# Image 0 in three transfers over 128 partitions, sums of the first cells by identity products, and zeros ahead of image 0

## The reference

```
# first layer
g    = relu(bn2(einsum('nchw,oc->nohw', x, wg1))).mean(axis=(2, 3))
xg0  = (relu(tanh(g @ wg2.T + bg2)) + beta)[0]            # of image 0 alone
p    = round(xg0[:31] / xg0.sum() * 96)                   # splits the channels among 32 filters
filt = basis[i] for channels between param[i] and param[i+1]
xp   = x.reshape(n, 96, 7, 8, 7, 8).mean(axis=(3, 5))     # 7 x 7 cells of 8 x 8 pixels
y    = relu(bn1((xp * filt).sum(axis=(2, 3)) @ w1d[:, :, 1].T + b1d))
x    = x * y + x
# second layer
t    = relu(gamma * (x.mean(axis=(2, 3)) @ w1.T - mean) * rsqrt(var + eps) + beta)
wt   = (t @ w2.T + b2) as 3 x 3 for each image and channel, masked to its first four taps
out  = depthwise conv of x with wt + bias
```

## Time and profile before

| | |
|---|---|
| time, median of 3 runs | 230.43 us (229.45 to 232.28) |
| profiled execution, time | 229.69 us |
| its span, first to last instruction | 227.5 us |
| mean granted TensorE clock | 0.954 of full speed |
| busy: PE, PEld | 206.4 us, 119.0 us |
| busy: DVE, ACT, POOL | 199.4 us, 132.4 us, 129.5 us |
| DMA | 79.05 MB, mean 348 GB/s |
| largest group | L740 PE, 480 records, 171.1 us |

### The profile page before, as it was taken

The page is one execution under the profiler, slowest core; times in us unless marked ns, Lnnn a source line. Parts: engine busy times, 40 slices in busy tenths (PEclk is TensorE's granted clock), DMA queues, the critical chain, the costliest instruction groups (busy, mean ns, idle before and its releaser), DMA issues.

```text
span 227.5 us, 2390 instructions
## 1 busy us (share of the span) xinstructions
PE 206.4 (91%) x742; PEld 119.0 (52%) x742; DVE 199.4 (88%) x216; ACT 132.4 (58%) x190; POOL 129.5 (57%) x121
## 2 busy tenths in 40 slices
PE   7291866999999999999999999999999999999991
PEld 3141453556556555655565656565556555655550
DVE  6036969997999999999999999989999999788983
ACT  2002115648765867586767677667766775687650
POOL 3004167998598669867886878696879400040000
PEclk9769585999999999999999999999999999999999
DMA  4999999869999999999999999999997246615676
GB/s 109 276 426 430 426 430 421 354 192 353 430 375 405 371 415 432 426 355 426 437 422 357 424 432 424 389 413 422 383 419 335 124 176 282 282 71 212 282 309 256
DMA packets 8155, 79.05 MB, mean 348 GB/s; under 512 B 1040, under 2 KB 1072, under 8 KB 2128
## 3 DMA queue, kind: packets, MB, share of 16 engines
q1 hardware_dynamic: 8144, 78.92, 86.7%
HBM read 40.38 MB, written 38.54 MB: 347 GB/s over the span
## 4 chain that ended last, share of the span: by engine, by line
PE 75%; DVE 10%; ACT 6%; DMA 3%; issue 2%; SPq 1%; DVEq 1%; ACTq 0%
PE banks L740 61%; DVE banks L550 6%; ACT banks L625 4%; PE banks L688 3%; DMA xout<-x 3%; PE banks L725 2%; PE banks L732 2%; PE banks L711 2%; PE banks L713 2%; DVE xout L550 2%; PE banks L675 1%; ACT diag L620 1%; DVE stats L425 1%; SPq L284 1%; PE banks L703 1%
## 5 line engine op out<-in xcount | busy, mean ns | idle before, releaser
L740 PE MATMUL banks<-xin,diag 128*128 128x385 f32 (+1 forms) x480 | 171.1, 507 | 3.0 <-ACT banks L625 2.7
L740 PEld LDWEIGHTS banks<-xin,diag 128*128 128x128 f32 x480 | 88.4, 192 | 68.4 <-issue 27.2
L339 POOL TENSOR_TENSOR halves<-xin 128x1568 f32<-128x1568 f32 (+2 forms) x22 | 74.1, 3371 | 43.9 <-DVE stats L438 21.3
L550 DVE SCALAR_TENSOR_TENSOR banks<-xin,coef,banks 128x1485 f32<-128x1485 f32 x48 | 84.8, 1768 | 6.9 <-ACT banks L625 6.3
L625 ACT ACTIVATE banks<-xin,wide_sb,coef 128x784 f32<-128x784 f32 (+2 forms) x71 | 84.3, 1207 | 10.6 <-DVE xout L559 8.8
L550 DVE SCALAR_TENSOR_TENSOR xout<-xin,coef,banks 128x1485 f32<-128x1485 f32 x24 | 42.2, 1758 | 0.6 <-issue 0.3
L646 ACT ACTIVATE xout<-banks 128x784 f32<-128x784 f32 x24 | 19.8, 824 | 39.2 <-PE banks L740 39.2
L344 POOL TENSOR_TENSOR halves<-halves 128x784 f32<-128x784 f32 x18 | 33.2, 1845 | 1.4
L620 ACT ACTIVATE diag<-wide_sb,coef 128x128 f32<-128x128 f32 x72 | 23.5, 389 | 5.9 <-DVE coef L484 5.9
L559 DVE SCALAR_TENSOR_TENSOR xout<-xin,coef,banks 128x825 f32<-128x825 f32 x24 | 25.6, 1067 | 1.0 <-PE banks L740 0.8
L366 POOL TENSOR_TENSOR edges<-xin,coef 128x84 f32<-128x84 f32 x24 | 8.3, 344 | 21.0 <-DVE coef L484 20.2
(11 more groups left out here) (72 smaller groups left out, 77.2 us busy)
## 6 DMA issues: line engine op xcount, KB each, us to landing
xin<-x SPq DMA_DIRECT2D x23, 1568.0 KB, 10.9
out<-xout SPq DMA_DIRECT2D x23, 1568.0 KB, 13.0
xout<-x SPq DMA_DIRECT2D x4, 294.0 KB, 5.3
xin<-x SPq DMA_DIRECT2D x1, 1120.0 KB, 14.6
out<-xout SPq DMA_DIRECT2D x1, 756.0 KB, 3.2
wide_sb<-wide SPq DMA_DIRECT2D x1, 499.5 KB, 16.0
xin<-x SPq DMA_DIRECT2D x1, 448.0 KB, 15.2
out<-xout SPq DMA_DIRECT2D x1, 420.0 KB, 3.3
```

The costliest lines, as they stand in the source:

```text
L339: eng.tensor_tensor(halves[:, j % 2, 0:end, :], cells[:, :, 0, :], cells[:, :, 1, :], ALU.add).then_inc(once_folded, 1)
L550: return vec.scalar_tensor_tensor(out=to, in0=grid(k)[:, irows, cols], scalar=weight(k, which), in1=d_rows[:, :, ocols], op0=ALU.mult, op1 ...
L740: return mm(to, diag[:, k % 2, which, :], grid(k)[:, irows, cols], start=False, stop=(which == LEFT), skip_group_check=True)
```

## The change

It does six things.

- Image 0 comes in three transfers, one for each third t of its channels, each into all 128 partitions: partition 4q + j holds quarter j of channel 3q + t. It is issued ahead of `early_sb`, behind `gate_one` and a piece of `wide`.
- `gate_one` is loaded four times over by a broadcast transfer (128 partitions of 948 bytes), the first 132 columns of `wide` (the identity and `quarter_of`, a 0/1 mask of partition mod 4) come in a transfer of their own (`ident_in`), and `gate_w` is made by three multiplies on VectorE instead of GpSimd's zeros and four copies. TensorE waits for transfer t ahead of its two products of t, not for all ahead of the first.
- Products of zeros before image 0: four instead of one. The two ahead of `mix(0)` go.
- Cell sums: `sum_rows` adds up the 8 pixel rows of a cell row by 8 products with the identity into a PSUM bank, and `sum_array` on VectorE adds up 8 columns at a time. It takes cell rows 0 to 3 of tile 1 (four products before `p_later`, four behind it) and 5 and 6 of tile 2 (behind the filter products). GpSimd now folds rows 4 to 6 of tile 1 and rows 0 and 1 of tile 2; VectorE sums rows 2 to 4 of tile 2 directly, and none of tile 1.
- ScalarE makes `seed_a(0)` before the three diagonals of tile 0, and each diagonal counts on `diag_done`, so that the first products of tile 0 wait for one diagonal at a time.
- Constants and offsets in `wide` move to fit.

```
@@ -41,7 +41,8 @@
 AHEAD = 5
 QUARTER = HW // 4
 GATE_HALF = QUARTER // 2
-HEAD_FOLDED = (0, 4, 3)
+CELLS_1, CELLS_2 = (0, 4), (5, 7)
+FOLDED_1, FOLDED_2 = (4, 7), (0, 2)
 HEAD_PART = 5
 ONCE = (4, 5)
 
@@ -97,7 +99,7 @@
 
     x_tiles = x.rearrange("n c h w -> (n c) (h w)").rearrange("(g p t) f -> g t p f", p=P, t=PER)
     out_tiles = out.rearrange("n c h w -> (n c) (h w)").rearrange("(g p t) f -> g t p f", p=P, t=PER)
-    x_image0 = x[0, :, :, :].rearrange("c h w -> c (h w)").rearrange("(q t) (j f) -> j q t f", t=PER, j=GROUP)
+    x_image0 = x[0, :, :, :].rearrange("c h w -> c (h w)").rearrange("(q t) (j f) -> t q j f", t=PER, j=GROUP)
 
     with ExitStack() as ctx:
         def sb(name, shape):
@@ -162,8 +164,9 @@
         w_tap = narrow_sb[:, N_TAP:N_END].rearrange("p (k c) -> p k c", k=TAPS)
         bias = wide_sb[:, W_BIAS:W_MIX]
         w_mix = wide_sb[:, W_MIX:W_HIDE].rearrange("p (t c) -> p t c", t=PER)
-        w_hid = wide_sb[0:C, W_HIDE:W_IDENT]
-        ident = wide_sb[:, W_IDENT:W_IMAGE]
+        w_hid = wide_sb[0:C, W_HIDE:W_IMAGE]
+        quarter_of = wide_sb[:, W_QUARTER:W_IDENT]
+        ident = wide_sb[:, W_IDENT:W_BIAS]
         image_of = wide_sb[:, W_IMAGE:W_PICK]
         pick = [wide_sb[:, W_PICK + (PER - 1 - t) * QUAD:W_PICK + (PER - 1 - t) * QUAD + C] for t in range(PER)]
         to_rows = wide_sb[0:C, W_SPREAD:W_END].rearrange("p (t r) -> p t r", t=PER)
@@ -278,10 +282,12 @@
 
         @block.sync
         def _(sp):
+            sp.dma_start(gate_one[:, :], early.rearrange("(q j t) e -> q j (t e)", j=1, t=PER).broadcast_to(
+                [QUAD, GROUP, PER * E_END])).then_inc(gate_one_in, 16)
+            sp.dma_start(wide_sb[:, 0:W_BIAS], wide[:, 0:W_BIAS]).then_inc(ident_in, 16)
+            for t in range(PER):
+                sp.dma_start(image0[:, t, :], x_image0[t]).then_inc(image0_in[t], 16)
             sp.dma_start(early_sb[:, :], early[:, E_GATE2:E_END]).then_inc(early_in, 16)
-            sp.dma_start(gate_one[:, :, :], early.rearrange("(q t) e -> q t e", t=PER)).then_inc(gate_one_in, 16)
-            for j in range(GROUP):
-                sp.dma_start(image0[QUAD * j:QUAD * (j + 1), :, :], x_image0[j]).then_inc(image0_in[j], 16)
             sp.dma_start(narrow_sb[:, :], narrow).then_inc(narrow_in, 16)
 
             def load(k, first=0, end=H):
@@ -296,7 +302,7 @@
             load(1).then_inc(loaded[1], 16)
             load(2, 0, HEAD_PART * BLK).then_inc(part_in, 16)
             load(2, HEAD_PART * BLK, H).then_inc(loaded[2], 16)
-            sp.dma_start(wide_sb[:, :], wide).then_inc(wide_in, 16)
+            sp.dma_start(wide_sb[:, W_BIAS:W_END], wide[:, W_BIAS:W_END]).then_inc(wide_in, 16)
             for k in range(PER, IN_BUFS):
                 load(k).then_inc(loaded[k], 16)
 
@@ -325,7 +331,6 @@
         @block.gpsimd
         def _(pool):
             eng = nc.gpsimd
-            eng.memset(gate_w[:, :, :], 0.0).then_inc(gate_zeroed, 1)
             eng.memset(expo[:, :], -0.5).then_inc(expo_set, 1)
             pool.wait_ge(expo_set, 1)
             pool.wait_ge(fold, 3)
@@ -333,10 +338,10 @@
             eng.tensor_tensor(rs_chan[:, :], b_chan[:, :], expo[0:C, :], ALU.pow).then_inc(rsqrt_done, 1)
             eng.tensor_tensor(rs_hid[:, :], b_hid[:, :], expo[0:HID, 0:1], ALU.pow).then_inc(rsqrt_done, 1)
 
-            def fold_once(j, end=DCT):
-
-                cells = xin[:, j % IN_BUFS, PAD:].rearrange("p (a h f) -> p a h f", a=DCT, h=2)[:, 0:end, :, :]
-                eng.tensor_tensor(halves[:, j % 2, 0:end, :], cells[:, :, 0, :], cells[:, :, 1, :],
+            def fold_once(j, first=0, end=DCT):
+
+                cells = xin[:, j % IN_BUFS, PAD:].rearrange("p (a h f) -> p a h f", a=DCT, h=2)[:, first:end, :, :]
+                eng.tensor_tensor(halves[:, j % 2, first:end, :], cells[:, :, 0, :], cells[:, :, 1, :],
                                   ALU.add).then_inc(once_folded, 1)
 
             def fold_twice(j):
@@ -385,6 +390,15 @@
             vec.memset(zeros[:, :], 0.0).then_inc(zeroed, 1)
             vec.memset(xin[:, :, 0:PAD], 0.0).then_inc(pad_zeroed, 1)
 
+            dve.wait_ge(gate_one_in, 16)
+            dve.wait_ge(ident_in, 16)
+            for t in range(PER):
+                vec.tensor_tensor(gate_w[:, t, :].rearrange("p (j o) -> p j o", j=GROUP),
+                                  gate_one[:, E_END * t:E_END * t + NF].rearrange("p (j o) -> p j o", j=1).broadcast_to(
+                                      [P, GROUP, NF]),
+                                  quarter_of.rearrange("p (j o) -> p j o", o=1).broadcast_to([P, GROUP, NF]),
+                                  ALU.mult).then_inc(gate_placed, 1)
+
             dve.wait_ge(early_in, 16)
             for j in range(GROUP):
                 vec.tensor_copy(gate_in[QUAD * j:QUAD * (j + 1), :], early_sb[0:NF, 0:E_HID - E_GATE2]).then_inc(gate_copied, 1)
@@ -392,12 +406,6 @@
             vec.tensor_scalar(b_hid[:, :], hid_par[:, 3:4], EPS, None, ALU.add).then_inc(fold, 1)
             dve.wait_ge(gate_copied, GROUP)
             vec.tensor_scalar(b_gate[:, :], gate_par[:, 3:4], EPS, None, ALU.add).then_inc(fold, 1)
-            dve.wait_ge(gate_zeroed, 1)
-            dve.wait_ge(gate_one_in, 16)
-            for j in range(GROUP):
-                vec.tensor_copy(gate_w[QUAD * j:QUAD * (j + 1), :, NF * j:NF * (j + 1)],
-                                gate_one[:, :, E_GATE1:E_GATE2]).then_inc(gate_placed, 1)
-
             dve.wait_ge(rsqrt_done, 1)
             vec.tensor_tensor(a_gate[:, :], gate_par[:, 0:1], rs_gate[:, :], ALU.mult).then_inc(fold, 1)
             dve.wait_ge(fold, 4)
@@ -426,10 +434,17 @@
                                          xin[:, j % IN_BUFS, PAD + first * BLK * W:PAD + end * BLK * W].rearrange(
                                              "p (a b c d) -> p a c b d", b=BLK, c=DCT, d=BLK), AX.XY, ALU.add)
 
-            def sum_once_folded(j, folds, end=DCT):
+            def sum_array(j, rows, bank, sums_before):
+
+                dve.wait_ge(array_cells, sums_before)
+                return vec.tensor_reduce(stats[:, 0, j % PER, rows[0] * DCT:rows[1] * DCT],
+                                         banks[:, bank, 0:(rows[1] - rows[0]) * W].rearrange("p (c d) -> p c d", d=BLK),
+                                         AX.X, ALU.add)
+
+            def sum_once_folded(j, folds, first=0, end=DCT):
 
                 dve.wait_ge(once_folded, folds)
-                return vec.tensor_reduce(cells_of(j, 0, end), halves[:, j % 2, 0:end, :].rearrange(
+                return vec.tensor_reduce(cells_of(j, first, end), halves[:, j % 2, first:end, :].rearrange(
                     "p a (b c d) -> p a c b d", c=DCT, d=BLK), AX.XY, ALU.add)
 
             def sum_twice_folded(j):
@@ -504,18 +519,16 @@
             dve.wait_ge(assign, 4)
             vec.scalar_tensor_tensor(out=hit[:, :], in0=chan, scalar=bounds[:, 1:2], in1=p_above,
                                      op0=ALU.is_lt, op1=ALU.mult).then_inc(hit_done, 1)
-            dve.wait_ge(loaded[1], 16)
-            sum_direct(1, HEAD_FOLDED[1], DCT)
+            sum_once_folded(1, 1, *FOLDED_1)
             dve.wait_ge(later_mm, 1)
 
             vec.scalar_tensor_tensor(out=chosen[:, :, :].rearrange("p t q -> p (t q)"), in0=p_later, scalar=0.5,
                                      in1=hit[:, :], op0=ALU.is_lt, op1=ALU.mult).then_inc(chosen_done, 1)
-            sum_once_folded(1, 1, HEAD_FOLDED[1]).then_inc(cells_done, 1)
             dve.wait_ge(part_in, 16)
-            sum_direct(2, HEAD_FOLDED[2], HEAD_PART)
-            dve.wait_ge(loaded[2], 16)
-            sum_direct(2, HEAD_PART, DCT)
-            sum_once_folded(2, 2, HEAD_FOLDED[2]).then_inc(cells_done, 1)
+            sum_direct(2, FOLDED_2[1], HEAD_PART)
+            sum_array(1, CELLS_1, BANK_D, 1).then_inc(cells_done, 1)
+            sum_once_folded(2, 2, *FOLDED_2)
+            sum_array(2, CELLS_2, BANK_D + 1, 2).then_inc(cells_done, 1)
             dve.wait_ge(mask_set, 1)
             dve.wait_ge(filt_mm, 1)
             weigh_cells(0)
@@ -617,8 +630,7 @@
             def diagonals(k):
                 act.wait_ge(coef_done, k // PER + 1)
                 for which in (LEFT_UP, RIGHT_UP, LEFT):
-                    ins = sca.activation(diag[:, k % 2, which, :], ident, ACT.Copy, scale=weight(k, which))
-                ins.then_inc(diag_done, 1)
+                    sca.activation(diag[:, k % 2, which, :], ident, ACT.Copy, scale=weight(k, which)).then_inc(diag_done, 1)
 
             def seed(k, acc, first, end):
                 act.wait_ge(loaded[k % IN_BUFS], 16 * (k // IN_BUFS + 1))
@@ -649,8 +661,9 @@
             lift_relu(0)
             hidden_relu(0)
             act.wait_ge(pad_zeroed, 1)
+            act.wait_ge(coef_done, 1)
+            seed_a(0)
             diagonals(0)
-            seed_a(0)
 
             for k in range(TILES):
                 g, t = k // PER, k % PER
@@ -674,15 +687,23 @@
```

(34 more changed lines are left out.)

115 lines of the change are left out of this document (70 added, 45 removed).

## The result

The changed kernel takes 228.33 us in the median of 20 runs (227.35 to 229.72), the kernel before 230.49 us (229.45 to 232.83, 20 runs) beside it on the same chip: a ratio of 0.9907, 95% interval 0.9883 to 0.9930. That is 2.2 us, or 0.9%, less, where 5.1 us were forecast. The time lies in the predicted range, but the gain is 2.2 us of the 5.1 us, and it is within the 2% that the chances call no difference. Some runs of the kernel before take 232.2 to 232.8 us (four of these 20, without which the difference is 2.0 us, and five of the 11 beside e5 to e8), and of the other kernels only one run of e8, which its ratio leaves out, so ratios of different sessions don't compare well. The profiled execution took 228.26 us (span 226.2 us, mean clock 0.962), 1.43 us less than the one of before.

What follows compares the result with a forecast made beforehand. Bound by the tap products' start (36.22 us) plus a 191 us body; weighing 3.6, coefficients 0.5 and seed 0.65 us give 4.75 us: 224.9 or 225.7 us, said 225.3 us; eight in ten 222.8 to 228.5 us.

Steps and rivals of the forecast that it cites:

- What bounds the kernel: Whole span: start of the tap products, 36.22 us, plus a body of 191 us; only the front can change.
- The loads queue behind: Loads after image 0: first lands near 10.5 instead of 14.0 us, later ones 3.5 us earlier, tile 1 at 14.2 us.
- the half rate: Image 0's transfer: 222 GB/s against 401 to 452, laid to writing 32 partitions, with short rows kept as rival.
- rival (1): Late loads: rate stays at 0.22 MB/us, tile 3 comes at 26.5 us as now; 226.9 us, chance 0.12.
- Zeros and image 0: TensorE's start: image 0's products from about 7.7 us, 3.9 us long, ended at 12.0 instead of 16.88 us.
- The cover of b_gate: Early constants behind image 0: b_gate 3.8 us later, at 9 us, still ahead of the products' end.
- The filter chain: Image 0's products to weighing, with TensorE's cell sums: count at 15.0 us, weighing 23.5 instead of 27.14 us, 3.6 us gained.
- up throughout: Filter chain with TensorE's clock up all along: p_later 17.2 us, weighing 22.3 us.
- down until 20.6 us: Filter chain with TensorE's clock down from 14.6 us: p_later 18.7 us, weighing 24.7 us.
- rival (3): Slower: TensorE at 1.2 GHz is the bound, weighing at 29.8 us; 231.7 us, or 27.4 us weighing with early loads; chance 0.05.
- rival (2): Identity sums: weight loads don't hide, 32 records cost 0.1 us more each, 3.2 us; 228.3 us, chance 0.11.
- To the first tap: Weighing to first tap: coefficients at 30.0 us, 0.65 us less by the seed, tap at 31.4 instead of 36.22 us.

Runs made afterwards that it cites:

- e5: e1 with image 0's three transfers issued ahead of gate_one and the wide piece; 227.10 us, 0.9815 to the kernel before.
- e8: The kernel before with only seed_a(0) put ahead of the three diagonals, each diagonal counted by itself; 228.56 us, 0.9872 to the kernel before.
- e1: The changed kernel with cell sums divided as before, none on TensorE, and the two zero products before mix(0) back; 226.36 us, 0.9829 to the kernel before.
- e2: The changed kernel, sums kept, with five more products of zeros in TensorE's waits behind image 0; 226.37 us, 0.9829 to the kernel before.
- e7: e1 with 128-column products of zeros behind the mixing, hiding and spreading products (2, 1 and 5); 227.02 us, 0.9792 to the kernel before.
- e9: e6 with zeros in all of TensorE's waits and two 512-column products of zeros behind the spreading ones; 226.43 us, 0.9808 to the kernel before.
- e11: The changed kernel with the three diagonals ahead of seed_a(0) again; 229.50 us, 0.9929 to the kernel before.
- e13: e9 without the zeros behind the spreading products; 227.79 us, 0.9858 to the kernel before.
- e12: e1 with the three diagonals ahead of seed_a(0) again; 227.74 us, 0.9841 to the kernel before.
- e6: e1 with total_step(0) ahead of tile 3's direct sums and gained_step(0) one sum earlier; 226.51 us, 0.9776 to the kernel before.
- e10: The kernel before with e9's zeros and seven more ahead of image 0's products, nothing else of the change; 227.11 us, 0.9838 to the kernel before.

## Why the prediction was wrong in size

**What bounds the kernel: right.** The span is the start of the taps plus a constant. The table holds it to 0.1 us over twelve kernels.

**The first step that failed: "The loads queue behind".** Tile 0 was forecast 3.5 us earlier, near 10.5 us, and came at 12.9 us, 1.1 us earlier; tile 1 at 16.7 instead of 14.2 us (issued 5.50 us, 11.2 us to landing). I had the bytes flow at 0.42 MB/us from 3.1 us. They begin to flow near 4 us, since image 0's issues stand behind two others (88 GB/s from 3 to 4 us), and go at 0.36 MB/us on average from 4 to 9 us; by the windows the 3.1 MB had moved at 11.5 us, which is 1.0 us of the 2.4 us. The other 1.4 us is a term that I put at nothing: the transfers issued behind tile 0 move beside it. When it landed, the engines had moved 3.7 MB, 0.6 MB of it for later tiles. The partitions were the better guess for the half rate: 128 partitions in the same 3136-byte rows gave 311 to 406 GB/s in the windows from 4 to 9 us, where 32 gave 198 to 295 from 5 to 10 us, so rival (1) is out, though no run changed the partitions alone. The Trainium skill, "SBUF — State Buffer", section "Door 1: The DMA port swizzle", has 32 neighbouring partitions on half of the ports; the trace agrees by its rates and still shows no ports.

**Zeros and image 0: right.** 7.35 us and 4.11 us, where 7.7 us and 3.9 us were said; ended at 11.46 instead of 12.0 us. The start is the early end of what the zeros allow: the same eight records, 2.80 us here, took 3.2 to 4.0 us in e1, e2, e5 to e7, e9 and e11 to e13, and image 0's products started at 8.07 to 8.85 us. It cost those kernels little, since xg waited for tile 0's sum. The cover of b_gate, costed at nothing, is down to 0.1 us: it is ready at 11.43 us (said: 9 us), the relu starts at 11.56 us. In e11, where it landed later, the relu waits for it until 12.45 us.

**The filter chain: the second error, in part from the first, and the larger one.** count at 16.1 instead of 15.0 us: with tile 0 late, its 2.02 us sum starts at 12.97 us and xg stands behind it on VectorE's queue from 13.2 to 14.91 us. I had not asked what the shorter chain would newly collide with. Then the sums. I had bounded TensorE's clock by "up throughout" (weighing 22.3 us) and "down until 20.6 us" (24.7 us) and taken the middle. It was down from 14.7 to 21.5 us, at the bad end, and tile 1 was 2.5 us late besides: weighing at 25.94 us, 1.2 us beyond the bound. Gained: 1.2 us of the 3.6 us forecast. (The reading that the clock held 5.7 us after image 0's products in the kernel before is wrong: it fell at 22.2 us, 5.3 us after them. The sum doesn't use it.) Undoing this part alone (e1, which also has its two zero products ahead of mix(0) back) gives 2.0 us by the medians and 1.44 us by the table, so it worked against the change. The step that failed is thus the middle taken between the bounds: the sums moved to TensorE ran at 1.2 GHz until 21.5 us, and tile 1's 16 records took 5.60 us (said: 3.0 us at full clock, 6.0 us at half), where e2 has 3.56 us at full clock. e1 has loads as late as the change and gains 4.1 us of the 5.1 us forecast, so the sums are the larger part of the miss; no run had early loads, and their part is argued. This is rival (3)'s mechanism, TensorE at 1.2 GHz as the bound; the weighing stayed short of the 27.8 us from which it would have made the kernel slower.

**Weight loads: rival (2) is out.** 2.04 us for 16 records is 0.13 us each, where 0.14 us was taken. A record of 224 columns takes 0.22 us at full clock (e2), by 0.19 us of its share of the 0.33 us for 392 columns; a load of weights, 0.19 us in the mean of the taps' line, can't stand between them. But the six filter records of 49 columns take 0.14 us each at full clock, no less than those of 112: a record has a floor here, of which the runs don't show whether it is the load's. The Trainium skill, "TensorE: Matmul & The Clock Gate", section "The mechanism" (the prediction names the section behind it), says that a load overlaps running products only when its row group differs; with all 128 rows in each record, e2's 0.22 us contradict it.

**To the first tap: right but for the clock.** From the weighing to the coefficients it is 7.4 us (25.94 to 33.35), taken at 6.5 us: make_taps ran at half clock (1.44 us). The seed's 0.65 us measured 0.46 to 0.55 us. The cold taps lost 1.80 us where the sum had the same 1.5 us as before.

**By parts**, on the table's sum: transfers and zeros 37.73 to 36.15 us (e12), 1.6 us; seed 0.5 us, and 0.4 us by e1's earlier tile 0; identity sums -1.4 us; together 1.0 us. With the 0.42 us between the two rests that makes the profiles' 1.43 us. The medians' 2.2 us is more, chiefly since the profiled run of before, 229.69 us, was 0.8 us faster than its median.

**Open.** What decides in which run the clock rises earlier, and so why e8's median gains more than its profile; and why the mixing records that make over half of the difference between the rests take longer in the kernels built on before. No combination of the best parts is clearly below 226.4 us: e1, e2, e6 and e9 lie within 0.2 us in their medians, with the fastest run at 224.8 us (e6).

## What to carry to other kernels

Work moved to a TensorE that has idled is done at the clock that it finds there: price it at half clock, and look whether cheap filler ahead of it (e2, e10) is worth more than the move itself. When a serial chain is shortened, list for each step of it what will now be queued ahead of it on an in-order engine. And for a kernel with a steady body, reduce each trial to one number, the start of the body plus what it loses cold; it says where a gain arises, which medians of a few runs don't, but it is one execution, with that execution's clock in it.

## What the runs showed that was not expected

Some 2 us pass between the first large issue and the full rate of the DMA engines: with image 0 issued from 2.05 us they moved 88 GB/s from 3 to 4 us and 348 GB/s from 4 to 5 us, and with image 0 issued first, at 0.73 us (e5), 386 GB/s from 3 to 4 us. The two issues ahead of it thus held image 0 back by 1.3 us, with 0.2 MB of their own.

Ten records of 128-column zeros ahead of the taps, at 0.25 us each without a pause, left the clock at 0.50 (e7), while with four records of 512 columns in that place, at about 0.9 us each, it was up within 1.1 us of the first tap in e9 and just ahead of it in e10. That the width made the difference isn't shown. From the start of the unbroken work to the rise it was 5.8 us in e7, 4.6 us in e9 and 3.2 us in e10, and with taps alone it was anything from 3.0 us (the kernel before) to 6.1 us (e6).
